# Second attention: the next group's scores in front of all four turned probabilities

## The chip, the cores and the metric

One core of one Trainium2 chip runs the whole kernel. The metric is the device time in microseconds (us) of one execution; lower is better. The engines are TensorE (matmuls), ScalarE (activations), VectorE and GpSimd (elementwise and reductions), and SyncE (issues most transfers). Each works through its own queue in order and waits on semaphores.

## The reference

Six layers are added to a state x of 16 batches x 64 tokens x 512 channels: a projected cross attention, a recurrent time mix, an FP4 feed-forward layer, a second cross attention without projections, a sparse self attention and a ternary feed-forward layer. The change touches the fourth:

```
q = layernorm(x), heads: 16 of 32 channels          # 64 tokens in each of 16 batches
k = v = ctx_1024, heads: 16 of 32 channels          # 512 keys in each of 16 batches
scores  = einsum('bhqd,bhkd->bhqk', q, k) / sqrt(32)
weights = softmax(scores, axis=-1)
x = x + einsum('bhqk,bhkd->bhqd', weights, v)
```

## The kernel before, in words

The layer is `cross_attention`. Its work is cut into 32 groups (`QUADS`), k = 0 to 31; batch b = k // 2, half = k % 2. A group is eight heads of one batch, held as four blocks r = 0 to 3 of 128 rows (two heads of 64 tokens each) by 512 keys; the title's "four heads" are these four blocks. For each group:

- `scores(k)` (matmul on L1116): 16 matmuls into four PSUM banks, one for each r. It waits until all four maxima of group k-1 are taken (`scored` at 4k), since they read the same banks.
- `scored_max(k)` on VectorE (L1250): four instructions, each copies a bank to SBUF (`l1x_prob`) and takes the row extremum (`l1x_negmax`). It waits for `scores(k)`.
- `exponential(k, r)` on ScalarE (L1201): one for each r, with the row sums, after the maximum of that r.
- `turn_probabilities(k, r)` on TensorE (L1131): four transposes of 128x128 into one of three banks, after exponential r and after the copy of the turn three before, which had the same bank.
- `turned_copy(k, r)`: the copy of a turned block to SBUF (`l1x_PT`), on ScalarE (L1209) for r = 0 and 2, and r = 1 of odd k; on VectorE (L1258) for r = 3, and r = 1 of even k.
- `half_product(k)` on TensorE (L1151): 64 small matmuls with the values, one group later.
- For odd k: `heads_copy` (ScalarE, L1214), `turn_back` (TensorE, L1161) and `finish_heads` (VectorE, L1273) of the batch before; GpSimd (L1101) adds the result to x.

The order in each queue is written out by hand in the loops over k. On ScalarE: exponentials 0 and 1, heads_copy (odd k), copy 0, exponential 2, copy 1 (odd k), exponential 3, copy 2. On VectorE: copy 3 of group k-1, finish_heads (odd k), copy 1 (even k), the four maxima of group k+1, and for every fourth k the moments of x. SyncE loads the keys of a batch (`l1x_KT`, three buffers, released by `score_full`) and the values (`l1x_ctx`, four buffers, released by `half_full`). The last group is followed by its half product, a turn_back and the first transposes for the next stage.

Of the kernel before, what the change touches and what calls it, by code (L numbers as in the profile page):

```python
# [461 lines left out]
def head_of(half, e, r):  # L462

    return 4 * (2 * half + e) + r
# [578 lines left out]
QUADS = 2 * B  # L1043
# [16 lines left out]
def cross_attention(nc, g, d, w, loads, zeros):  # L1060
# [19 lines left out]
    with nc.Block() as block:  # L1080
        @block.sync
        def _(sp):
            context_loads(d, w, (2, 3))(sp)
            for b in range(B):
                if b + 3 < B:
                    sp.wait_ge(score_full, 2 * (b + 1))
                    sp.dma_start(w.KT[b % 3][:, :, :], d.ctxT[b + 3]).then_inc(keys_loaded[b % 3], 16)
                if b + 4 < B:
                    sp.wait_ge(half_full, 2 * b + 2)
                    sp.dma_start(w.ctx[b % 4][:, :, :], ctx_dram[b + 4]).then_inc(ctx_loaded[b % 4], 16)  # L1090
            loads(sp)
# [11 lines left out]
        @block.tensor  # L1103
        def _(pe):
            def scores(k):

                b, half = k // 2, k % 2
                if half == 0:
                    pe.wait_ge(keys_loaded[b % 3], 16 * (b // 3 + 1))
                if k > 0:  # L1110
                    pe.wait_ge(scored, 4 * k)
                for e in range(2):
                    c = 2 * half + e
                    for r in range(4):
                        rows = slice(32 * r, 32 * r + 32)
                        last = nc.tensor.matmul(score[r][e * T:(e + 1) * T, :], w.QT[rows, c, b * T:(b + 1) * T],  # L1116
                                                w.KT[b % 3][rows, c, :], start=True, stop=True)
                last.then_inc(score_full, 1)

            def turn_probabilities(k, r):  # L1120

                n = 4 * k + r
                if n == 2:
                    pe.wait_ge(last_summed, 1)
                pe.wait_ge(exp_done, n + 1)
                if n >= 3:
                    pe.wait_ge(scalar_copied, SCALAR_COPIES[n - 3])
                    if VECTOR_COPIES[n - 3] > 0:
                        pe.wait_ge(vector_copied, VECTOR_COPIES[n - 3])
                for kc in range(KC):  # L1130
                    last = nc.tensor.transpose(probt[n % 3][:, kc * P:(kc + 1) * P], prob(k, r)[:, kc * P:(kc + 1) * P],  # L1131
                                               g.ident[:, :])
                last.then_inc(probt_full, 1)

            def half_product(k):

                b, half = k // 2, k % 2
                pe.wait_ge(scalar_copied, SCALAR_COPIES[4 * k + 3])
                pe.wait_ge(vector_copied, VECTOR_COPIES[4 * k + 3])
                if k == 0:  # L1140
                    pe.wait_ge(last_copied, 1)
                if half == 0:
                    pe.wait_ge(ctx_loaded[b % 4], 16 * (b // 4 + 1))
                    if b > 0:
                        pe.wait_ge(heads_done, b)
                for e in range(2):
                    c = 2 * half + e
                    for kc in range(KC):
                        for r in range(4):
                            h = head_of(half, e, r)  # L1150
                            last = nc.tensor.matmul(pv[32 * r:32 * r + 32, c * T:(c + 1) * T],  # L1151
                                                    w.ctx[b % 4][:, kc, h * HD:(h + 1) * HD],
                                                    turned(k, r)[:, kc * P + e * T:kc * P + (e + 1) * T],
                                                    start=kc == 0, stop=kc == KC - 1)
                last.then_inc(half_full, 1)

            def turn_back(b):

                pe.wait_ge(heads_out, b + 1)
                for half in range(2):  # L1160
                    last = nc.tensor.transpose(pv[:, 256 + half * P:256 + (half + 1) * P],  # L1161
                                               w.headsT[b % 2][:, half * P:(half + 1) * P], g.ident[:, :])
                last.then_inc(heads_back, 1)

            def turn_last_rows():

                pe.wait_ge(last_normed, 1)
                for c in range(CH):
                    ins = nc.tensor.transpose(pv[:, c * P:(c + 1) * P], g.XN[:, final, c * P:(c + 1) * P], g.ident[:, :])
                ins.then_inc(last_turned, 1)  # L1170

            scores(0)
            for k in range(QUADS):
                turn_probabilities(k, 0)
                turn_probabilities(k, 1)
                if k % 2 == 1 and k > 1:
                    turn_back(k // 2 - 1)
                if k + 1 < QUADS:
                    scores(k + 1)
                turn_probabilities(k, 2)  # L1180
                turn_probabilities(k, 3)
                if k > 0:
                    half_product(k - 1)
                else:
                    turn_last_rows()
            half_product(QUADS - 1)
            turn_back(B - 1)
            pe.wait_ge(scored, 4 * QUADS)
            for t in range(EARLY_TILES):
                pe.wait_ge(normed, t + 1)  # L1190
                for c in range(CH):
                    last = nc.tensor.transpose(score[t][:, c * P:(c + 1) * P], g.XN[:, t, c * P:(c + 1) * P], g.ident[:, :])
                last.then_inc(rows_turned, 1)
# [2039 lines left out]
```

## Time and profile before

| | |
|---|---|
| median of 3 runs | 1519.95 us (1519.93 to 1522.32) |
| time of the profiled execution | 1521.73 us |
| its span, first to last instruction | 1519.9 us |
| TensorE busy over the span | 1415.1 us (93%) |
| VectorE busy | 1106.7 us (73%) |
| ScalarE busy | 620.1 us (41%) |
| GpSimd busy | 176.2 us (12%) |
| mean granted TensorE clock | 0.986 |
| this stage, about | from 1112 to 1285 us |

The busy times are averages over six stages with different limits; a matmul's end is modelled, so a busy TensorE is not one at its peak. What this stage is limited by can only be read inside its stretch. Times in the timeline count from the span's start; entries of one kind that follow each other are merged, with their count behind an x. "issue" is idle time that nothing in the profile released.

### The profile page before, as it was taken

The numbers are of one execution on the slowest core, as the hardware profiler recorded it, in microseconds if no ns is written. First come the engines' busy times: TensorE is split into PE (matmuls) and PEld (weight loads), VectorE is DVE, ScalarE is ACT, GpSimd is POOL, SyncE is SP. The second block draws the span as 40 slices with busy tenths as digits, with TensorE's granted clock in tenths as the row PEclk, the third lists the DMA queues.
The fourth block names the chain that finished last, engine by engine and source line by source line (L and its number), as shares of the span: only waits on it lengthen the run. The fifth ranks groups of instructions, "written<-read, shape, count | busy, mean of one in ns | idle before, by whom it ended". The sixth has DMA issues, their size and how long they took to land. (4 is left out here: it accounts for less than half of the span.)

```text
span 1519.9 us, 33229 instructions
## 1 busy us (share of the span) xinstructions
PE 1415.1 (93%) x13858; PEld 929.3 (61%) x13858; DVE 1106.7 (73%) x2270; ACT 620.1 (41%) x1289; POOL 176.2 (12%) x171
## 2 busy tenths in 40 slices
PE   8999999999999999899979999999989998978898
PEld 5677777777777777434555644444446655667454
DVE  5577777877888788774565887677668777675787
ACT  2455444544544444111223411111178886134543
POOL 3300000000000000031000000000000001253800
PEclk9999999999999999899999999999999999999999
DMA  7353444444545543500006200000045563300000
GB/s 260 129 176 136 143 139 157 148 143 143 170 148 166 166 136 101 166 1 1 2 3 229 112 1 0 0 0 0 0 167 210 190 229 99 110 3 2 1 28 28
DMA packets 55449, 153.65 MB, mean 101 GB/s; under 512 B 11997, under 2 KB 16861, under 8 KB 49162
## 3 DMA queue, kind: packets, MB, share of 16 engines
q1 hardware_dynamic: 50186, 134.82, 26.0%
q0 software_dynamic: 5120, 16.78, 2.8%
q8 instruction: 107, 1.75, 0.5%
q14 instruction: 36, 0.29, 0.1%
HBM read 117.73 MB, written 33.85 MB: 100 GB/s over the span
## 5 line engine op out<-in xcount | busy, mean ns | idle before, releaser
L805 ACT ACTIVATE l0x_prob<-l0x_prob,l0x_negmax 128x512 f32<-128x512 f32 x128 | 90.9, 712 | 110.3 <-DVE l0x_negmax L881 110.2
L663 PE MATMUL bank<-l0x_upper_v,l0x_ctxT 128*128 128x512 f32 x256 | 106.6, 417 | 2.1 <-DVE l0x_V L860 2.1
L650 PE MATMUL bank<-l0x_ctxT,l0x_upper_k 128*128 128x512 f32 x256 | 106.7, 417 | 1.3 <-PEq L272 1.3
L665 PE MATMUL bank<-l0x_upper_v,l0x_ctxT_lower 128*128 128x512 f32 x256 | 101.6, 397 | 0.0
L664 PE MATMUL bank<-l0x_lower_v,l0x_ctxT 128*128 128x512 f32 x256 | 101.3, 396 | 0.0
L652 PE MATMUL bank<-l0x_ctxT,l0x_lower_k 128*128 128x512 f32 x256 | 100.7, 393 | 0.0
L651 PE MATMUL bank<-l0x_ctxT_lower,l0x_upper_k 128*128 128x512 f32 x256 | 100.2, 391 | 0.0
L2180 ACT ACTIVATE f_silu<-bank 128x512 f32<-128x512 f32 (+1 forms) x24 | 13.5, 561 | 190.4 <-PE bank L2107 190.4
L1201 ACT ACTIVATE l1x_prob<-l1x_prob,l1x_negmax 128x512 f32<-128x512 f32 x128 | 91.0, 715 | 0.0
L1131 PE MATMUL bank<-ident,l1x_prob 128*128 128x128 f32 x512 | 78.6, 288 | 13.2 <-ACT l1x_prob L1201 9.0
L1250 DVE CUSTOM_DVE_ANT_0 l1x_prob<-bank,l1x_zeros 128x512 f32<-128x512 f32 x128 | 80.8, 687 | 13.3 <-PE bank L1116 13.3
L608 POOL DMA_DIRECT2D turned_context<-l0x_whole x60 | 32.9, 548 | 475.6 <-ACT l0x_whole L783 475.6
L1131 PEld LDWEIGHTS bank<-ident,l1x_prob 128*128 128x128 f32 x512 | 55.6, 143 | 50.9 <-ACT l1x_prob L1201 41.7
L881 DVE CUSTOM_DVE_ANT_0 l0x_prob<-bank,l0x_mask 128x512 f32<-128x512 f32 x128 | 80.7, 687 | 3.8 <-PE bank L678 3.8
L2107 PE MATMUL bank<-f_gateT,f_x 128*128 128x512 f32 (+1 forms) x192 | 79.7, 558 | 1.4 <-ACT f_x L2172 1.4
L798 ACT ACTIVATE l0x_KT<-bank,columns 128x512 f32<-128x512 f32 x64 | 43.8, 684 | 91.0 <-PE bank L652 91.0
L2107 PE MATMUL bank<-f_upT,f_x 128*128 128x512 f32 (+1 forms) x192 | 79.5, 557 | 0.0
L2157 PE MATMUL bank<-f_downT,f_hT 128*128 128x512 f32 x154 | 67.4, 593 | 0.6 <-ACT f_hT L2191 0.6
L815 ACT ACTIVATE l0x_PT<-bank 128x512 f32<-128x512 f32 x128 | 65.9, 610 | 2.1 <-PE bank L687 2.1
L663 PEld LDWEIGHTS bank<-l0x_upper_v,l0x_ctxT 128*128 128x128 f32 x256 | 48.7, 190 | 24.5 <-issue 13.8
L650 PEld LDWEIGHTS bank<-l0x_ctxT,l0x_upper_k 128*128 128x128 f32 x256 | 48.1, 188 | 23.6 <-issue 14.2
L687 PE MATMUL bank<-ident,l0x_prob 128*128 128x128 f32 x512 | 62.3, 273 | 0.2
(339 smaller groups left out, 3091.7 us busy)
## 6 DMA issues: line engine op xcount, KB each, us to landing
l0x_ctx<-in_ctx SPq DMA_DIRECT2D x16, 1024.0 KB, 5.3
turned_context<-l0x_whole POOLq DMA_DIRECT2D x64, 256.0 KB, 2.4
l1x_KT<-turned_context SPq DMA_DIRECT2D x16, 1024.0 KB, 7.4
l1x_ctx<-in_ctx SPq DMA_DIRECT2D x16, 1024.0 KB, 4.9
fp_weight<-l0x_weight_piece SPq DMA_DIRECT2D x24, 352.0 KB, 4.8
f_raw<-fp_weight SPq DMA_DIRECT2D x3, 2816.0 KB, 18.3
l0x_abs_piece<-in_L_ffn_w_gate SPq DMA_DIRECT2D x16, 512.0 KB, 4.9
l0x_abs_piece<-in_L_ffn_w_up SPq DMA_DIRECT2D x16, 512.0 KB, 5.5
```

Of the source, the lines that this page charges most:

```text
L650: nc.tensor.matmul(bank[:, :], w.upper_k[:, kc, cols], c, start=kc == 0, stop=False)
L651: nc.tensor.matmul(bank[:, :], w.upper_k[:, kc, cols], c_lower, start=False, stop=False)
L652: last = nc.tensor.matmul(bank[:, :], w.lower_k[:, kc, cols], c, start=False, stop=kc == CH - 1)
L663: nc.tensor.matmul(bank[:, :], c, w.upper_v[:, kc, :], start=kc == 0, stop=False)
L664: nc.tensor.matmul(bank[:, :], c, w.lower_v[:, kc, :], start=False, stop=False)
L665: last = nc.tensor.matmul(bank[:, :], c_lower, w.upper_v[:, kc, :], start=False, stop=kc == CH - 1)
L805: nc.scalar.activation(w.prob[r][:, :], w.prob[r][:, :], ACT.Exp, scale=-1.0, bias=w.negmax[:, p:p + 1], accum_out=w.rowsum[:, b % 2, p:p ...
L881: nc.vector.tensor_tensor_reduce(w.prob[r][:, :], score[r][:, :], w.mask[b % 2][:, :], 1.0, 3e38, ALU.add, ALU.min, w.negmax[:, p:p + 1]). ...
L1131: last = nc.tensor.transpose(probt[n % 3][:, kc * P:(kc + 1) * P], prob(k, r)[:, kc * P:(kc + 1) * P], g.ident[:, :])
L1201: nc.scalar.activation(prob(k, r)[:, :], prob(k, r)[:, :], ACT.Exp, scale=-1.0, bias=w.negmax[:, p:p + 1], accum_out=w.rowsum[:, b % 4, p: ...
L1250: nc.vector.tensor_tensor_reduce(prob(k, r)[:, :], score[r][:, :], w.zeros[:, :], 1.0, 3e38, ALU.add, ALU.min, w.negmax[:, p:p + 1]).then_ ...
L2107: last = nc.tensor.matmul(bank[:, 0:n], w.x[:, kc, :], weight[:, kc, at:at + n], start=kc == 0, stop=kc == CH - 1)
```

## The change

In TensorE's loop the call `scores(k + 1)` moves from behind turns 0 and 1 of group k (and turn_back) to the front of the iteration. Each waits for what it waited for before; ScalarE's, VectorE's, SyncE's and GpSimd's queues keep their order.

```
             scores(0)
             for k in range(QUADS):
+                if k + 1 < QUADS:
+                    scores(k + 1)
                 turn_probabilities(k, 0)
                 turn_probabilities(k, 1)
                 if k % 2 == 1 and k > 1:
                     turn_back(k // 2 - 1)
-                if k + 1 < QUADS:
-                    scores(k + 1)
                 turn_probabilities(k, 2)
                 turn_probabilities(k, 3)
                 if k > 0:
```

## Rows read from the trace of the kernel before

**Rows 1.** Windows over the second attention: stretch, length, busy us (count) by engine, clock, DMA.
```profile
...
1112.00:1285.00 173.00, 152.01 (x3126) 100.90 (x3127) 136.17 (x376) 145.05 (x361) 12.65 (x11) 0.98 0.51 184
```

**Rows 2.** Waits in the same stretch: us in total, times, longest.
```profile
...
ACT l1x_PT L1209 <- PE bank L1131: 17.9, 27, 2.6
DVE l1x_prob L1250 <- PE bank L1116: 13.3, 31, 2.1
```

**Rows 3.** Timeline of TensorE (start us, us, line, operation, count, idle before).
```profile
...
1129.17 1.11 PE L1116 MATMUL bank<-l1x_KT,XNT 32*64 32x512 f32 x16
...
1163.24 1.09 PE L1131 MATMUL bank<-ident,l1x_prob 128*128 128x128 f32 x8
1164.17 0.38 PE L1161 MATMUL bank<-ident,l1x_headsT 128*128 128x128 f32 x2
1164.48 1.11 PE L1116 MATMUL bank<-l1x_KT,XNT 32*64 32x512 f32 x16
1165.53 0.66 PE L1131 MATMUL bank<-ident,l1x_prob 128*128 128x128 f32 x4
1166.47 0.66 PE L1131 MATMUL bank<-ident,l1x_prob 128*128 128x128 f32 x4 [0.29 <-ACT l1x_prob L1201]
1167.06 1.10 PE L1151 MATMUL bank<-l1x_PT,l1x_ctx 128*32 128x64 f32 x64
1168.09 1.09 PE L1131 MATMUL bank<-ident,l1x_prob 128*128 128x128 f32 x8
1169.11 1.11 PE L1116 MATMUL bank<-l1x_KT,XNT 32*64 32x512 f32 x16
...
1173.71 1.11 PE L1116 MATMUL bank<-l1x_KT,XNT 32*64 32x512 f32 x16
...
1270.37 1.11 PE L1116 MATMUL bank<-l1x_KT,XNT 32*64 32x512 f32 x16
```

**Rows 4.** The same timeline, a stall and the product behind it.
```profile
...
1201.15 0.92 PE L1131 MATMUL bank<-ident,l1x_prob 128*128 128x128 f32 x7 [1.88 <-issue]
1202.00 1.93 PE L1151 MATMUL bank<-l1x_PT,l1x_ctx 128*32 128x64 f32 x64
```

**Rows 5.** Timeline of ScalarE in the undisturbed pair.
```profile
...
1165.13 0.58 ACT L1209 ACTIVATE l1x_PT<-bank 128x512 f32<-128x512 f32 x1
1165.61 0.72 ACT L1201 ACTIVATE l1x_prob<-l1x_prob,l1x_negmax 128x512 f32<-128x512 f32 x1
...
1168.78 0.60 ACT L1209 ACTIVATE l1x_PT<-bank 128x512 f32<-128x512 f32 x1 [0.47 <-PE bank L1131]
1169.28 0.71 ACT L1201 ACTIVATE l1x_prob<-l1x_prob,l1x_negmax 128x512 f32<-128x512 f32 x1
...
1169.98 0.71 ACT L1201 ACTIVATE l1x_prob<-l1x_prob,l1x_negmax 128x512 f32<-128x512 f32 x1
```

**Rows 6.** Timeline of VectorE in the undisturbed pair.
```profile
...
1164.66 0.86 DVE L1273 TENSOR_TENSOR l1x_heads<-bank,l1x_rinv 64x256 f32<-64x256 f32 x2 [1.08 <-PE bank L1161]
...
1169.22 0.69 DVE L1258 COPY l1x_PT<-bank 128x512 f32<-128x512 f32 x1 [0.38 <-PE bank L1131]
1170.33 0.69 DVE L1250 CUSTOM_DVE_ANT_0 l1x_prob<-bank,l1x_zeros 128x512 f32<-128x512 f32 x1 [0.42 <-PE bank L1116]
...
1172.78 0.69 DVE L1258 COPY l1x_PT<-bank 128x512 f32<-128x512 f32 x1
```

**Rows 7.** Timeline of all engines in the last stage.
```profile
...
1426.23 0.75 DVE L2929 SCALAR_TENSOR_TENSOR f_h<-bank,f_worth,f_silu 128x512 f32<-128x512 f32 x1
...
1427.04 1.64 PE L2782 MATMUL bank<-f_gateT,f_x16T 128*128 128x512 bf16 x4 [2.67 <-DVE f_h L2929]
```

**Rows 8.** Windows, as in rows 1, of three stretches.
```profile
...
760.00:780.00 20.00, 14.62 (x558) 11.87 (x561) 11.01 (x18) 4.83 (x7) 0.00 (x0) 1.00 0.01 3
780.00:800.00 20.00, 14.23 (x385) 10.84 (x375) 17.08 (x34) 5.25 (x17) 0.00 (x0) 0.83 0.01 4
1200.00:1210.00 10.00, 8.85 (x176) 6.98 (x176) 6.21 (x19) 7.00 (x18) 1.28 (x1) 0.83 0.52 190
```

More of the change, by code:

```diff
@@ L1173, in _ @@
             for k in range(QUADS):
+                if k + 1 < QUADS:
+                    scores(k + 1)
                 turn_probabilities(k, 0)
@@ L1177, in _ @@
                     turn_back(k // 2 - 1)
-                if k + 1 < QUADS:
-                    scores(k + 1)
                 turn_probabilities(k, 2)
```

## The prediction

> **What bounds the kernel now.** I read the windows of the trace first, for the stage that the change touches. The second attention takes 173 us, 11.4% of the span. In it TensorE is busy 152 us, ScalarE 145 us and VectorE 136 us, at a granted clock of 0.98 [rows 1]: no engine is full, three are close, so the order of one group's steps sets the time. The list of waits comes next: ScalarE's copies wait 17.9 us for turned probabilities, VectorE's maxima 13.3 us for scores [rows 2]. Then TensorE's timeline. An undisturbed pair of groups (an even and an odd one) takes 1173.71 - 1164.48 = 9.23 us from one score block to the one two groups on; the 28 groups from the score block at 1129.17 to that at 1270.37 take 141.2 us, and 14 x 9.23 = 129.2 us, so 12.0 us are disturbance [rows 3]. Of what kind, TensorE's rows show: 1.88 us of "issue" (nothing in the profile released it), and behind it a product of 64 matmuls that takes 1.93 us where its like takes 1.10 us [rows 3, 4]; the window from 1200 to 1210 us has a mean granted clock of 0.83, so part of it ran at the lower level of 1.2 GHz [rows 8].
>
> In the undisturbed pair TensorE's own pitches are 1.05 us for a score block (1164.48 to 1165.53), 1.02 us for two turned heads (1168.09 to 1169.11), 1.03 us for a half product (1167.06 to 1168.09), 0.31 us for turn_back (1164.17 to 1164.48) [rows 3]. Twice (1.05 + 2 x 1.02 + 1.03) plus 0.31 is 8.55 us of the 9.23: TensorE hardly waits, because scores(k+1) stands between turns 1 and 2. While TensorE runs that block, ScalarE copies turn 0 and does exponential 2, VectorE copies turn 1 (even k) or finishes heads (odd k). These are hidden behind 1.05 us of scores.
>
> **The change part by part.** No instruction is added or removed. 31 score blocks of 16 matmuls move ahead of two turns (eight transposes); nothing moves on ScalarE, VectorE, SyncE or GpSimd. It costs by what now waits on what. I write t for the time from the start of a moved score block, scores(k+1).
>
> New wait: this block needs all four maxima of group k. They were complete long before it when it followed turns 0 and 1; now turns 0 and 1 of group k, which need only exponentials 0 and 1, are queued behind that wait, and behind them the rest of TensorE, ScalarE's copy 0 with exponentials 2 and 3 after it, and VectorE's copy 1 with the maxima of group k+1 after it.
>
> Even k, through VectorE. Turn 0 starts at 1.05. VectorE's copy of turn 1 starts 1.13 after turn 0 (1168.09 to 1169.22 [rows 3, 6]), at 2.18. It has the maxima's duration, 0.69, and I give it their pitch, 0.61 (a quarter of 2.45, below [rows 6]), so the four maxima start at 2.79. The scores themselves would have let them start at 1.22 (1169.11 to 1170.33 [rows 3, 6]): the earlier scores buy nothing, since the maxima are queued behind the copy. Four maxima have a pitch of 2.45 in all (1170.33 to 1172.78), the last starts 1.84 after the first and takes 0.69 [rows 6]. From a VectorE result to a TensorE start that waited for it no row of this stage speaks; the nearest is of the last stage, 1426.23 + 0.75 to 1427.04, 0.06 us [rows 7]. Bounds are 0 and 0.17 (ScalarE's exponential of 0.71 us, released to its turn 0.86 after its start, 1165.61 to 1166.47, is 0.15 past its end [rows 3, 5]); I take 0.06. First maximum to next score block: 1.84 + 0.69 + 0.06 = 2.59. Sum 5.38 us.
>
> Even k, through ScalarE. Copy 0 starts 0.69 after turn 0 (1168.09 to 1168.78), exponential 2 after 0.50, exponential 3 after 0.70 [rows 3, 5], turn 3 after 0.86, half product after 0.59 (1166.47 to 1167.06), the next score block 1.03 later: 1.05 + 0.69 + 0.50 + 0.70 + 0.86 + 0.59 + 1.03 = 5.42 us. The two loops are nearly equal; the longer counts, 5.42.
>
> Odd k, through VectorE. Turn_back starts 0.93 after turn 0 (1163.24 to 1164.17), finish_heads 0.49 later (1164.66), which takes 0.86 [rows 3, 6], then the maxima: 1.05 + 0.93 + 0.49 + 0.86 + 2.59 = 5.92 us. Through ScalarE the extra copy of turn 1 costs 0.48 (1165.13 to 1165.61 [rows 5]): 5.90 us. I take 5.92.
>
> A pair is then 11.34 us against 9.23, +2.11, and 14 pairs take 158.8 us. Both loops would have to be wrong for it to be less; with ScalarE's alone it is 11.32.
>
> The disturbances: 12.0 us before. TensorE now idles 11.34 - 8.55 = 2.79 us of each pair, so part of a stall falls into idle time, and it consumes instructions slower. Bounds are 0 (all hidden) and 12.0 (none); with a quarter of the time idle and stalls of up to 1.88 us against idle pieces of about 1 us, I take half, 6.
>
> The ends: four of the 32 groups lie outside the 28. Bounds are 1.0 us (only the two turns that now stand behind the last scores) and 4 x 2.11 / 2 = 4.2 us; the first groups have no turn_back and no half product of the group before, so I take 2.7.
>
> Transfers: a keys load is issued on a score block's end and used four groups later, about 18 us; an order moved by two turns (1.02 us) leaves that cover. Adds on GpSimd wait for finished heads only and are not waited for in the loop. Cost 0; if the cover were gone, TensorE would stand at the first score block of a batch, at most the 1.02 us moved, sixteen times.
>
> Sum: 158.8 + 6 - 141.2 + 2.7 = +26.3 us. The profiled execution has a span of 1519.9 us and its own time is 1521.73 us, 1.8 above the median of the runs, 1519.95; its sum would be 1548.0, and on the median 1546.3 us. I give the latter.
>
> **A rule weighed.** The transposes run at full clock here: the stage has a granted clock of 0.98 though two turned heads alternate with everything else [rows 1, 3]. The Trainium skill, page "TensorE: Matmul & The Clock Gate", Part 4, says that a transpose "doesn't count as PE-busy the same way" and that full clock does not engage for it. In this trace the rule does not show. By it the changed order, with 2.08 us of other matmuls left in 5.67, would sink to half clock, and the time would be that of the low clock rival below, the whole stage of it; since the trace speaks against the rule, it adds 0.02 to that rival's chance and no more (in the 0.10 below).
>
> **The rivals.**
> Low clock: TensorE's busy share falls to 8.55 / 11.34 = 75%. For it: the stretch 780 to 800 us has 14.2 us busy of 20 and a clock of 0.83. Against it: the stretch 760 to 780 us has 14.6 of 20 and a clock of 1.00 [rows 8], and the new idle pieces are about 1 us each. Price: at the lower clock a half product takes 1.93 us for 1.10 [rows 3, 4], a factor of 1.75; on the loop that adds 0.79 for scores, 0.38 each for turns 0 and 3 and 0.77 for the product, 2.3 us a group. A third of 28 groups gives +21, that is 1568 us; the whole stage +64. It decides from the point where the granted clock of the stage falls under about 0.9.
>
> No change: ScalarE's load would stay the bound (145 of 173 us) and the new wait be covered. That wants both loops of 5.4 to 5.9 us to be under 4.6, a whole score block less in each. Time 1520 us.
>
> Faster: one mechanism, VectorE's waits for scores. The 13.3 us [rows 2] vanish since scores come two turns earlier, the exponentials follow, and TensorE never waits for them: 1519.95 - 13.3 = 1506.7 us. It decides from the point where the maxima of k+1 may start at 1.22 and not 2.79 after the scores; the code's order on VectorE puts copy 1 or finish_heads in front, so only if these did not depend on turns issued behind the scores. They do.
>
> Half the loss: stalls vanish altogether and the ends cost 1.0: 158.8 - 141.2 + 1.0 = +18.6, and slack that I do not see (a shorter release, engines running ahead after each stall) takes another 5 to 8: about 1532 us.
>
> **How the numbers follow.** The forecast, with its own range from the bounds (+18.6 to 158.8 + 12 - 141.2 + 4.2 = +33.8: 1538.6 to 1553.8), 0.76. Low clock 0.10, half the loss 0.09, no change 0.03, faster 0.02. The range 1535 to 1558 takes the forecast's, some of the half loss and the mildest low clock: about 0.82. Changes under 0.2% (3 us) can't be told from none here. So faster 0.02, same 0.03, slower 0.95.
>
> **What would show it.** In the changed kernel's trace TensorE's score blocks lie 5.4 (even) and 5.9 us (odd) apart; before a score block TensorE waits for VectorE's maximum, a wait that is not in the list now, at least in odd groups; VectorE's maxima start 2.8 us after the score block and no longer wait for it, its copies and finish_heads wait for TensorE instead; ScalarE idles about 1.5 us before each copy 0. Sums of durations stay; the stage is about 199 us long. I am wrong if the score blocks lie under 5.2 us apart, if the granted clock of the stage falls under 0.9, or if time appears outside this stage.

## The result

The changed kernel takes 1544.54 us (median of 4 runs, 1541.35 to 1548.80) against 1520.93 us: a ratio of 1.0145, 95% interval 1.0129 to 1.0161, which is +22.1 us (19.6 to 24.5). The two medians by themselves are 23.6 us apart, inside that interval. The forecast was 1546.3 us, slower.

The windows of the kernel before, cut at the first score block of the stage, at that of the 4th group, at the last score block and at the stage's end; the fourth row is all that comes behind the stage (us, then busy us by engine in the order TensorE, its weight loads, VectorE, ScalarE, GpSimd, then clock, share of the DMA engines, GB/s):

```profile
...
1112.50:1129.17 16.67, 11.88 (x156) 7.14 (x157) 11.80 (x33) 12.30 (x29) 2.38 (x3) 0.90 0.67 253
1129.17:1270.37 141.20, 129.47 (x2717) 85.67 (x2716) 114.02 (x314) 121.89 (x309) 8.97 (x7) 0.99 0.54 195
1270.37:1284.47 14.10, 10.12 (x254) 7.77 (x253) 9.82 (x29) 10.86 (x25) 1.27 (x1) 1.00 0.01 3
1284.47:1519.90 235.43, 205.56 (x2240) 132.73 (x2240) 169.06 (x320) 87.15 (x124) 81.31 (x58) 0.98 0.11 37
```

The same windows of the changed kernel, cut at the same instructions:

```profile
...
1114.09:1132.63 18.54, 13.17 (x148) 7.64 (x149) 11.80 (x33) 11.76 (x27) 2.38 (x3) 0.72 0.57 227
1132.63:1292.17 159.54, 127.85 (x2723) 83.86 (x2716) 112.53 (x314) 121.17 (x310) 8.95 (x7) 1.00 0.48 173
1292.17:1308.34 16.17, 11.21 (x265) 8.64 (x261) 10.28 (x30) 11.37 (x27) 1.26 (x1) 1.00 0.01 3
1308.34:1547.00 238.66, 208.56 (x2240) 133.20 (x2240) 168.99 (x320) 87.10 (x124) 81.39 (x58) 0.96 0.11 37
```

The stage grew from 172.0 to 194.3 us, +22.3. The 28 groups in the middle give +18.3 (141.20 to 159.54), the first groups +1.9 and the tail behind the last scores +2.1. Busy times in the middle are nearly the same (TensorE 129.5 and 127.9 us), so nothing got more expensive: the engines wait. The granted clock of the middle is 1.00. The other 4.8 us by which this execution is longer lie outside the stage (1.6 ahead of it, 3.2 behind it), on the same instructions. This execution is the slowest of the four; of the 23.6 us between the medians the stage's 22.3 leave 1.3. The part behind the stage took 235.4 us at a granted clock of 0.98 in the kernel before and in e7 and e8 below, 238.6 to 238.9 at 0.96 here and in e1, e2 and e3, and 240.9 at 0.95 in e12, whose stage is the shortest of all; so its length doesn't go with that of the stage, and what sets it was not tested.

The list of waits of the changed kernel over the stage (us in total, times, longest):

```profile
...
ACT l1x_PT L1209 <- PE bank L1131: 43.2, 32, 2.6
PE bank L1131 <- ACT l1x_prob L1201: 35.3, 48, 1.0
DVE l1x_PT L1258 <- PE bank L1131: 26.8, 18, 3.3
DVE l1x_heads L1273 <- PE bank L1161: 17.1, 9, 1.9
...
PE bank L1116 <- DVE l1x_negmax L1250: 3.3, 1, 3.3
```

ScalarE's copies wait 43.2 us for turns instead of 17.9 [rows 2]; VectorE's copies and finish_heads now wait 26.8 and 17.1 us. VectorE's maxima wait for scores once more only, at the start (1.7 us; 13.3 us before [rows 2]): they now stand behind those copies. TensorE's timeline over an even and an odd group of the changed kernel:

```profile
...
1280.78 1.12 PE L1116 MATMUL bank<-l1x_KT,XNT 32*64 32x512 f32 x16
1281.82 1.09 PE L1131 MATMUL bank<-ident,l1x_prob 128*128 128x128 f32 x8
1283.87 1.36 PE L1131 MATMUL bank<-ident,l1x_prob 128*128 128x128 f32 x8 [0.95 <-ACT l1x_prob L1201]
1285.16 1.10 PE L1151 MATMUL bank<-l1x_PT,l1x_ctx 128*32 128x64 f32 x64
1286.23 1.12 PE L1116 MATMUL bank<-l1x_KT,XNT 32*64 32x512 f32 x16
1287.28 1.09 PE L1131 MATMUL bank<-ident,l1x_prob 128*128 128x128 f32 x8
...
1289.32 0.66 PE L1131 MATMUL bank<-ident,l1x_prob 128*128 128x128 f32 x4 [0.73 <-ACT l1x_prob L1201]
1290.51 0.66 PE L1131 MATMUL bank<-ident,l1x_prob 128*128 128x128 f32 x4 [0.53 <-ACT l1x_prob L1201]
1291.10 1.10 PE L1151 MATMUL bank<-l1x_PT,l1x_ctx 128*32 128x64 f32 x64
1292.17 1.12 PE L1116 MATMUL bank<-l1x_KT,XNT 32*64 32x512 f32 x16
```

The reader compares with [rows 3]: there a wait stands only in front of turn 3 (0.29 us); here TensorE waits 0.95 us for exponential 2 in each even group and 0.73 and 0.53 us in each odd one. From score block to score block it is 5.45 us (even k) and 5.94 us (odd k). ScalarE's copies 0 of the same pair, and VectorE's copy 1 (1282.95), finish_heads (1288.70), first and last maxima:

```profile
...
1282.52 0.60 ACT L1209 ACTIVATE l1x_PT<-bank 128x512 f32<-128x512 f32 x1 [1.55 <-PE bank L1131]
...
1287.97 0.60 ACT L1209 ACTIVATE l1x_PT<-bank 128x512 f32<-128x512 f32 x1 [1.14 <-PE bank L1131]
```

```profile
...
1282.95 0.69 DVE L1258 COPY l1x_PT<-bank 128x512 f32<-128x512 f32 x1 [1.04 <-PE bank L1131]
1283.56 0.68 DVE L1250 CUSTOM_DVE_ANT_0 l1x_prob<-bank,l1x_zeros 128x512 f32<-128x512 f32 x1
...
1285.39 0.69 DVE L1250 CUSTOM_DVE_ANT_0 l1x_prob<-bank,l1x_zeros 128x512 f32<-128x512 f32 x1
...
1288.70 0.86 DVE L1273 TENSOR_TENSOR l1x_heads<-bank,l1x_rinv 64x256 f32<-64x256 f32 x2 [1.90 <-PE bank L1161]
1289.59 0.69 DVE L1250 CUSTOM_DVE_ANT_0 l1x_prob<-bank,l1x_zeros 128x512 f32<-128x512 f32 x1
...
1291.42 0.69 DVE L1250 CUSTOM_DVE_ANT_0 l1x_prob<-bank,l1x_zeros 128x512 f32<-128x512 f32 x1
```

The first maximum starts 2.78 us after the score block (1283.56 - 1280.78), though the scores are there after 1.2. In the odd group the last maximum (1291.42, 0.69 long) ends 0.06 us before the next score block; the half product in front of that block started 1.07 us before it, where its pitch is 1.03: both loops close within hundredths of a microsecond. In the even group the last maximum (1285.39, 0.69 long) ends 0.15 us before the next block (1286.23).

### The profile page after: what moved, and what is told of

Read it like the earlier page. It is cut to its first block and busy times, and to the rows that moved or that the text cites. A ratio compares the mean times of both kernels' runs of the same rounds, so it can differ in the third digit from the quotient of the medians.

```text
span 1547.0 us, 33229 instructions
## 1 busy us (share of the span) xinstructions
PE 1421.0 (92%) x13858; PEld 929.0 (60%) x13858; DVE 1105.7 (71%) x2270; ACT 619.4 (40%) x1289; POOL 176.4 (11%) x171
## 5 line engine op out<-in xcount | busy, mean ns | idle before, releaser
L1131 PE MATMUL bank<-ident,l1x_prob 128*128 128x128 f32 x512 | 78.6, 288 | 36.1 <-ACT l1x_prob L1201 35.3
L1209 ACT ACTIVATE l1x_PT<-bank 128x512 f32<-128x512 f32 x80 | 47.6, 594 | 43.8 <-PE bank L1131 43.2
## 6 DMA issues: line engine op xcount, KB each, us to landing
f_raw<-fp_weight SPq DMA_DIRECT2D x3, 2816.0 KB, 18.3
```

## The experiments

All ratios are to the kernel before, run on the same chip; it took 1521.2 to 1522.9 us there, up to 2 us more than in the comparison above, so experiments are compared with each other by ratio and by pair, not by time. "28 groups" is the time from the 4th group's score block to the last one; "disturbed" is what is left of it after 14 undisturbed pairs.

| kernel | pair (even + odd), us | 28 groups | disturbed | ratio (95%) |
|---|---|---|---|---|
| before | 9.23 | 141.2 | 12.0 | 1 |
| changed | 5.45 + 5.94 | 159.5 | 0.1 | 1.0145 (1.0129 to 1.0161) |
| e1_maxima_first | 5.41 + 5.94 | 159.4 | 0.5 | 1.0139 (1.0107 to 1.0172) |
| e2_exp2_first | 5.46 + 5.94 | 159.5 | 0.0 | 1.0136 (1.0105 to 1.0166) |
| e3_both | 4.71 + 5.94 | 150.0 | 0.9 | 1.0073 (1.0049 to 1.0097) |
| e4_wait_alone | 4.83 + 5.05 | 138.4 | 0.1 | 1.0004 (0.9989 to 1.0020) |
| e5_no_loads_before | 9.21 | 129.0 | 0.1 | 0.9901 (0.9878 to 0.9925) |
| e6_no_loads_changed | 11.40 | 159.6 | 0.0 | 1.0158 (1.0141 to 1.0175) |
| e7_between_turns | 5.02 + 5.51 | 147.4 | 0.0 | 1.0041 (1.0025 to 1.0056) |
| e8_product_earlier | 8.98 | 137.9 | 12.2 | 0.9965 (0.9949 to 0.9981) |
| e9_finish_between | 4.71 + 5.19 | 140.4 | 1.8 | 1.0000 (0.9983 to 1.0017) |
| e10_spread_loads | 9.21 | 144.0 | 15.0 | 1.0041 (1.0027 to 1.0055) |
| e11_spread_and_product | 8.98 | 135.5 | 9.8 | 0.9973 (0.9962 to 0.9983) |
| e12_apart_and_product | 8.98 | 125.7 | 0.0 | 0.9896 (0.9877 to 0.9915) |

### One loop or two: e1, e2, e3

e1, VectorE's queue of the changed kernel:

```
                 if k > 0:
                     turned_copy(k - 1, 3)
+                if k + 1 < QUADS:
+                    scored_max(k + 1)
                 if k % 2 == 1 and k > 1:
                     finish_heads(k // 2 - 1)
                 if not copied_by_scalar(k, 1):
                     turned_copy(k, 1)
-                if k + 1 < QUADS:
-                    scored_max(k + 1)
```

> The changed kernel, with VectorE's four maxima of group k+1 put in front of finish_heads (odd k) and of copy 1 (even k). Theory A (two loops tie, one through VectorE of 5.38 and 5.92 us, one through ScalarE of 5.42 and 5.90 us): only the VectorE loop is shortened, to 1.22 + 2.59 = 3.8 us; the ScalarE loop keeps the pair at 11.3 to 11.4 us, the time stays at 1543 to 1546 us. Rival B (the wait for the maxima alone makes the loss, ScalarE only follows): the pair falls to about 9.9 us, the time to 1522 to 1530 us.

Measured: a pair of 11.35 us, 1545.95 us. Shortening the loop through VectorE alone gains next to nothing. The even group of 5.41 us is ScalarE's loop by itself (5.42 worked out). The odd group of 5.94 us is not quite that: the edit puts finish_heads behind the maxima, and that makes a new loop of 5.94 us, 0.04 more than ScalarE's 5.90 (more on it under e3). TensorE still waits 0.73 and 0.53 us for exponentials in it, as in the changed kernel.

e2, ScalarE's queue of the changed kernel:

```
-                turned_copy(k, 0)
                 exponential(k, 2)
+                turned_copy(k, 0)
```

> The changed kernel, with ScalarE's exponential 2 put in front of copy 0. Theory A: only the loop through ScalarE is shortened, by 0.70 us a group, to 4.7 and 5.2 us; the loop through VectorE keeps the pair at 11.3 us, the time stays at 1542 to 1545 us. Rival C (ScalarE's chain copy 0, exponential 2, exponential 3, turn 3, half product alone makes the loss): the pair falls to 9.9 us, the time to 1522 to 1530 us.

Measured: 5.46 + 5.94 = 11.40 us, 1543.40 us. This is VectorE's loop by itself. Shortening ScalarE's loop alone gains nothing either, but the wait moves into sight. In the changed kernel TensorE waited for a maximum in front of scores once (3.3 us); in e2:

```profile
...
PE bank L1116 <- DVE l1x_negmax L1250: 23.4, 30, 3.3
```

e3 has both edits.

> The changed kernel with both orders changed: maxima first on VectorE, exponential 2 before copy 0 on ScalarE. Theory A: now both loops are shorter and the pair falls to 9.9 us (ScalarE loop 4.72 and 5.20 us), which takes 14 x 1.48 = 21 us and some 2 us at the ends off 1544.5, to about 1522 us, plus what comes back of TensorE's issue stalls (0 to 12 us): 1521 to 1533 us. Rival D (a score block in front of the turns costs its own 1.05 us a group whatever stands behind it): the pair stays at 9.23 + 2.1 = 11.3 us and the time at 1544 us.

Measured: 4.71 + 5.94 = 10.65 us (9.9 expected), 1532.51 us. The even group falls to the 4.72 us worked out for it: there each of the two loops alone had held it up. The odd group doesn't move. TensorE's timeline of e3 (odd group from 1195.28 to 1201.22):

```profile
...
1195.28 1.11 PE L1116 MATMUL bank<-l1x_KT,XNT 32*64 32x512 f32 x16
...
1200.19 1.10 PE L1151 MATMUL bank<-l1x_PT,l1x_ctx 128*32 128x64 f32 x64 [0.67 <-DVE l1x_heads L1273]
1201.22 1.11 PE L1116 MATMUL bank<-l1x_KT,XNT 32*64 32x512 f32 x16
...
1205.93 1.11 PE L1116 MATMUL bank<-l1x_KT,XNT 32*64 32x512 f32 x16
```

The product waits 0.67 us for `l1x_heads`: finish_heads, now behind four maxima, holds back the half product of the next batch, which writes into the same bank. This is a third loop, 1.22 + 2.45 + 0.24 + 0.86 + 0.14 + 1.03 = 5.94 us, and the edit made it: in the changed kernel finish_heads stands in front of the maxima, ends at 1289.56 and is not what the product at 1291.10 waits for.

### The third loop cut: e9

e9 is e3 with finish_heads between the second and third maximum (`scored_max` takes the blocks it is to do):

```
+                if k + 1 < QUADS:
+                    scored_max(k + 1, range(2))
                 if k % 2 == 1 and k > 1:
                     finish_heads(k // 2 - 1)
+                if k + 1 < QUADS:
+                    scored_max(k + 1, range(2, 4))
                 if not copied_by_scalar(k, 1):
                     turned_copy(k, 1)
```

> The changed kernel with exponential 2 before copy 0 and the maxima first on VectorE, but finish_heads between the second and the third maximum. With all four maxima in front of finish_heads, odd groups stayed at 5.94 us since half_product waited for finish_heads (1.22 + 2.45 + 0.24 + 0.86 + 0.14 + 1.03). Theory A: this third loop is cut, odd groups fall to 5.2 us (ScalarE's loop), the pair from 10.64 to 9.9 us, the time by 10 us to 1520 to 1525 us. Rival D (a score block in front costs its own 1.05 us): no fall under the 10.6 us.

Measured: 4.71 + 5.19 = 9.90 us, 1523.44 us, ratio 1.0000. With the scores still in front of all four turns, the loss in time is gone. In the loop it is not gone: the pair stays 0.67 us above the 9.23 of the kernel before, 9.4 us in 28 groups, which is ScalarE's shortened loop (4.72 + 5.20); that the time comes out even is because only 1.8 of the 12 us of disturbance are left. 1.49 of the 2.16 us of loss a pair went with three edits that leave the score block where it is, so that much is the price of what is queued behind it on the other two engines, and rival D (2.1 us a pair whatever stands behind) falls.

### The wait alone, and half the way: e4, e7

e4, TensorE's queue of the kernel before:

```
             for k in range(QUADS):
+                if k + 1 < QUADS:
+                    pe.wait_ge(scored, 4 * (k + 1))
                 turn_probabilities(k, 0)
```

> The kernel before, scores left where they were; only the wait for all four maxima of group k is put in front of turn 0 of group k, where the changed kernel has it. Theory A: VectorE's copy 1 and finish_heads are still hidden behind the score block, so the loop is turns 1.02 + first maximum 1.22 + 2.59 = 4.83 us (even) and 5.14 us (odd, with turn_back), a pair of 9.97 us, that is +0.74 x 14 = 10 us with the ends about 11; if the slack swallows the issue stalls of 12 us as it did in the changed kernel, the time is 1519 to 1523 us, if not up to 1532. Rival B (the wait alone makes the loss): a pair of 11.4 us and 1544 us.

Measured: a pair of 9.88 us. TensorE's timeline:

```profile
...
1163.68 1.11 PE L1116 MATMUL bank<-l1x_KT,XNT 32*64 32x512 f32 x16
...
1168.51 1.11 PE L1116 MATMUL bank<-l1x_KT,XNT 32*64 32x512 f32 x16
...
1172.32 1.09 PE L1131 MATMUL bank<-ident,l1x_prob 128*128 128x128 f32 x8 [0.40 <-DVE l1x_negmax L1252]
...
1173.56 1.11 PE L1116 MATMUL bank<-l1x_KT,XNT 32*64 32x512 f32 x16
```

From 1163.68 to 1168.51 it is the 4.83 us worked out for an even group, from 1168.51 to 1173.56, with turn_back in it, 5.05 (5.14 worked out), and the new wait is seen at 1172.32. Undisturbed, the wait costs 0.65 us a pair, 9 us in 28 groups; the disturbances of 12 us are gone with it, and the time is that of the kernel before (1.0004), so rival B falls. The other 1.51 us of the changed kernel's pair come with the scores standing in front of the turns.

e7 puts scores(k+1) between turn 0 and turn 1 of the kernel before:

```
                 turn_probabilities(k, 0)
+                if k + 1 < QUADS:
+                    scores(k + 1)
                 turn_probabilities(k, 1)
                 if k % 2 == 1 and k > 1:
                     turn_back(k // 2 - 1)
-                if k + 1 < QUADS:
-                    scores(k + 1)
```

> The kernel before with scores(k+1) between turn 0 and turn 1, halfway to the changed order. Theory A: VectorE loop with t from turn 0: even 0.51 + 1.05 to turn 1, copy 1 at 2.18, first maximum at 2.79, next score block at 5.38 and turn 0 0.51 earlier: 4.87 us; odd the same with turn_back 5.4 us; a pair of 10.3 us, +1.1. If the slack swallows the 12 us of stalls: 14 x 10.3 = 144 against 141.2 us, with the ends +4 to +5 us: 1523 to 1527 us. Rival D (the loss is the block's own 1.05 us in front of turn 0): no loss of the pair, 9.23 us, and 1520 us.

Measured: score blocks of e7 at

```profile
...
1154.90 1.12 PE L1116 MATMUL bank<-l1x_KT,XNT 32*64 32x512 f32 x16 [0.42 <-DVE l1x_negmax L1250]
...
1160.41 1.12 PE L1116 MATMUL bank<-l1x_KT,XNT 32*64 32x512 f32 x16
...
1165.43 1.12 PE L1116 MATMUL bank<-l1x_KT,XNT 32*64 32x512 f32 x16 [0.42 <-DVE l1x_negmax L1250]
```

5.51 us (odd) and 5.02 us (even), a pair of 10.53 us, 1529.69 us. TensorE waits 0.42 us for a maximum in front of the block that ends each even group. Half the way costs more than half the loss (1.30 of 2.16 us), and more than was expected (10.3 us and 1523 to 1527 us); rival D (9.23 us) falls. The even group is 0.15 us longer than worked out (4.87). 0.09 of that is the release: the last maximum ends 0.15 us before the block at 1165.43 (1164.59, 0.69 long), not 0.06. The rest was not looked into.

### Where the 12 us of disturbance went: e5, e6

e5 takes the loads of keys and values out of the kernel before, e6 out of the changed one; the waits stay, and the two waits on the loads are for the first load of each buffer:

```
                 if b + 3 < B:
                     sp.wait_ge(score_full, 2 * (b + 1))
-                    sp.dma_start(w.KT[b % 3][:, :, :], d.ctxT[b + 3]).then_inc(keys_loaded[b % 3], 16)
                 if b + 4 < B:
                     sp.wait_ge(half_full, 2 * b + 2)
-                    sp.dma_start(w.ctx[b % 4][:, :, :], ctx_dram[b + 4]).then_inc(ctx_loaded[b % 4], 16)
```

> The kernel before without the 25 loads of keys and values that SyncE issues inside the loop of the second attention (batches 3 and up read the keys of earlier ones, 4 and up the values; this part of the computation is left out, all waits on score and product blocks stay). It asks what the 12 us of issue stalls are. Theory E (TensorE's instructions arrive late because 1 MB loads share the DMA engines): no stalls, score blocks at 1129 and 1270 us lie 129 to 131 us apart, the time is 1508 to 1511 us. Rival F (they are TensorE outrunning its own supply, whatever else is moved): 141 us apart and 1520 us.

Measured: 129.0 us for the 28 groups and no "issue" in front of any matmul of them, 1510.25 us. The stalls come with the loads, and rival F falls.

> The changed kernel without the same 25 loads of keys and values inside the second attention (that part of the computation is left out). Its trace shows no issue stalls that the loads could have caused, so both theories of the stalls say: pair 11.4 us, time unchanged at 1542 to 1546 us. A fall by more than 3 us would say that the loads cost something in the new order after all.

Measured: 159.6 us for the 28 groups, as in the changed kernel; 1547.52 us (1.5 above the range expected), ratio 1.0158 (1.0141 to 1.0175), whose interval overlaps that of the changed kernel. In the middle of the changed order the loads cost nothing.

What the gaps are can be read further from their places. Counted through TensorE's program from the first score matmul, the nine gaps marked "issue" in the kernel before stand in front of matmuls 414, 538, 786, 1158, 1408, 1531, 2152, 2277 and 2524, from the first all whole steps of 124 (within three). Those of e8 and e10 stand on the same grid, and so do the few that are left in e1, e3 and e9. The DMA queue of the instructions in the kernel before over the stage (packets, MB, share of the time of 16 engines):

```profile
...
q8 instruction: 25, 0.41, 1.0%
```

25 packets for the 3126 matmuls and 3127 weight loads [rows 1] are one for 125 matmuls. So the gaps stand a whole number of packets apart, at nine of the 22 such places in the 28 groups, as late instructions would. The nine last 8.2 us together; the rest of the 12 us is slower work behind them.

### A faster kernel: e8, e10, e11, e12

e8, TensorE's queue of the kernel before:

```
                 turn_probabilities(k, 2)
-                turn_probabilities(k, 3)
                 if k > 0:
                     half_product(k - 1)
-                else:
+                turn_probabilities(k, 3)
+                if k == 0:
                     turn_last_rows()
```

> The kernel before with half_product(k-1) between turns 2 and 3 and not behind turn 3. The kernel before waits 0.3 to 0.5 us a pair for exponential 3 in front of turn 3, and ScalarE 0.67 us for turn 0 behind the product. The product fills that wait: the pair falls from 9.23 to 8.7 to 8.9 us (ScalarE is busy 8.67 us of it), 14 x 0.4 = 6 us less; 1513 to 1517 us if the stalls stay as they are. Rival G: with less slack the stalls grow by as much, and the time stays at 1521 us.

Measured: 8.98 us a pair (8.7 to 8.9 expected), 1518.12 us, 12.2 us of stalls, ratio 0.9965. A gain of 3.5 us in the loop, where 6 were expected; rival G falls.

e10 cuts each load in four and issues the parts over the pair (TensorE's waits on the loads count the parts):

```
+                for j in range(4):
...
+                    if b > 0 and b + 3 < B:
+                        sp.wait_ge(exp_done, 4 * (2 * b + (2, 3, 3, 4)[j]) + (4, 2, 4, 2)[j] - 4)
...
+                    for c in (2 * j % 4, 2 * j % 4 + 1):
+                        if j < 2 and b + 3 < B:
+                            sp.dma_start(w.KT[b % 3][32 * c:32 * c + 32, :, :], d.ctxT[b + 3][32 * c:32 * c + 32]).then_inc(keys_loaded[b % 3], 16)
```

> The kernel before with each 1 MB load of keys or values cut into four of 256 KB (32 partitions each, so packets keep their size), issued two at a time at four points of a pair, about two exponentials (2 us) apart, where one load of keys and one of values went out together. The same bytes. Theory E1 (a burst delays TensorE's instructions, and shorter bursts delay them less than its slack): stalls fall from 12 to 0 to 6 us, score blocks 1129 to 1270 lie 129 to 135 us apart, 1509 to 1516 us. Rival E2 (it is the bytes in flight over the stage that count, or the wait for one packet in each of the queues): 141 us apart, 1521 us.

Measured: 144.0 us for the 28 groups, stalls of 15.0 us, 1528.05 us, worse than either theory said. The DMA queue over the stage (packets, MB, share of the time of 16 engines), in the kernel before and in e10:

```profile
...
q1 hardware_dynamic: 10480, 31.36, 49.6%
```

```profile
...
q1 hardware_dynamic: 11680, 31.37, 78.2%
```

The same bytes hold the engines for 78% of the time instead of 50%. A part of 256 KB takes 5.0 (values) to 6.2 us (keys) to land, a whole of 1024 KB takes 4.9 to 7.4, all medians. The cut hardly shortened a burst, it filled the gaps between them.

> The same spread loads together with half_product(k-1) between turns 2 and 3, which by itself gave a pair of 8.98 us with 12.2 us of stalls left over 28 groups. If E1 holds: 14 x 8.98 + 0 to 6 = 126 to 132 us for the 28 groups, 1505 to 1512 us, the fastest of all. If E2 holds: 138 us and 1516 us.

Measured: ratio 0.9973 (0.9962 to 0.9983), 1518.06 us, 135.5 us for the 28 groups, 9.8 us of stalls: between the two theories, and not told apart from e8. E1 falls.

e12 is e8 with whole loads, but one after the other:

```
                     sp.wait_ge(score_full, 2 * (b + 1))
+                    sp.wait_ge(exp_done, 8 * (b + 1))
```

> half_product(k-1) between turns 2 and 3, as in the fastest kernel so far (0.9965 of the kernel before, pair 8.98 us, 12.2 us of stalls), and the keys load of a batch waits for the exponentials of group 2b+1, so that it goes out a group (4.6 us) apart from the values load and not 0.4 us from it. Loads stay whole, so their share of the DMA engines should stay near 50% (cutting them raised it to 78% and the stalls did not fall). Theory E3 (a stall needs two loads stacked in front of the instruction transfer): stalls fall to 0 to 6 us, ratio 0.989 to 0.994. Rival E2 (one load in flight is enough): stalls stay at 9 to 14 us, ratio 0.995 to 0.998.

Measured: 125.7 us for the 28 groups, which is 14 x 8.98 with nothing left; 1507.39 us, ratio 0.9896 (0.9877 to 0.9915), faster than both kernels. The DMA engines were busy 65% of the 28 groups, against 54% in the kernel before, and not near 50% as expected; so it is not the share of time or the bytes in flight that make the stalls, and rival E2 falls. SyncE's issues in the kernel before (one pair's worth) and in e12:

```profile
...
1203.97 0.33 SPq L1090 DMA_DIRECT2D l1x_ctx<-in_ctx  x1
1204.35 0.43 SPq L1087 DMA_DIRECT2D l1x_KT<-turned_context  x1
```

```profile
...
1195.99 0.33 SPq L1088 DMA_DIRECT2D l1x_KT<-turned_context  x1
1201.30 0.33 SPq L1091 DMA_DIRECT2D l1x_ctx<-in_ctx  x1
1204.97 0.33 SPq L1088 DMA_DIRECT2D l1x_KT<-turned_context  x1
```

A values load and a keys load went out 0.38 us apart and then nothing for most of a pair; now they are 3.7 to 5.3 us apart. The stage is 15.7 us shorter than in the kernel before (156.3 us for 172.0); this execution gave 5.5 us of that back behind the stage (240.9 us for 235.4), at the granted clock of 0.95 named above. TensorE's timeline of e12, with the product in front of turn 3 and no wait between:

```profile
...
1181.59 0.66 PE L1132 MATMUL bank<-ident,l1x_prob 128*128 128x128 f32 x4
1182.18 1.10 PE L1152 MATMUL bank<-l1x_PT,l1x_ctx 128*32 128x64 f32 x64
1183.21 1.79 PE L1132 MATMUL bank<-ident,l1x_prob 128*128 128x128 f32 x12
```

## Why the prediction was right

**The two loops.** Even 5.42 worked out, 5.45 measured; odd 5.92 and 5.94; pair 11.34 and 11.39; 14 pairs 158.8 and 159.5 us. The sum through VectorE and that through ScalarE were said to be nearly equal. e1, e2 and e3 show it for the even group: 5.41 us with ScalarE's loop alone, 5.46 with VectorE's alone, 4.71 with neither. For the odd group e2 shows VectorE's alone (5.94); ScalarE's 5.90 is seen in TensorE's waits for exponentials, and that neither is left at 5.19 us is shown by e9, since e1 and e3 had made a third loop of their own. One choice between the two was the wrong way round: in even groups the prediction let ScalarE's 5.42 count over VectorE's 5.38. The release of 0.06 us from a maximum to the score block, taken from the last stage, was 0.06 in odd groups (1291.42 + 0.69 to 1292.17) and 0.15 in even ones (1285.39 + 0.69 to 1286.23), inside its bounds of 0 and 0.17 (the two rows named for 0.17 give 0.14); with 0.15 VectorE's loop is 5.47 and the longer one. The error of 0.09 was covered by the tie.

**The disturbances** are the term that was mis-sized: I kept 6 of 12 us, and none were left in the 28 groups. The argument with idle pieces of about 1 us against stalls of up to 1.88 left too much. In e4 a pair of 9.88 us is already enough to lose them all, in e9 one of 9.90 us keeps 1.8 us. That alone accounts for -6 us.

**The ends** were 3.9 us for the 2.7 taken (bounds 1.0 and 4.2). The tail's 2.1 us is the same with and without loads (16.17 us in e6). A part of the opening's 1.9 is clock: its granted clock went from 0.90 to 0.72. e6, the same order without the loads, has an opening 1.4 us shorter at 0.90:

```profile
...
1111.88:1129.00 17.12, 10.77 (x149) 6.07 (x149) 11.79 (x33) 11.76 (x27) 2.37 (x3) 0.90 0.47 185
```

TensorE stands 3.3 us for the first maxima in both, and 3.1 us for the first exponential in the kernel before at 0.90, so that stand alone doesn't make the low clock; what does stays open.

Together: 18.3 + 3.9 = +22.3 us before rounding, for the +26.3 forecast. The medians are 23.6 us apart, so some 1.3 us lie outside the stage, and the kernel before took 1520.93 us and not the 1519.95 the forecast started from. These two, 2.3 us, hide part of the 4 us by which the stage was overestimated: 1544.5 against 1546.3 is closer than the sum deserves.

**The rivals.** Low clock: the middle ran at 1.00 with TensorE busy 80% of it, so it fell for the loop; only the opening, 19 us long, was lower (0.72). By the rule of the Trainium skill that it was weighed with (page "TensorE: Matmul & The Clock Gate", Part 4, on transposes) the clock would have sunk; the middle of this stage does not agree with it, at 1.00. Half the loss had its stalls right (they vanished) and no slack beside: the loops are as long as worked out. No change and faster fell with the loops; the maxima do start 2.78 us after the scores, behind copy 1, and putting them first (e1) does not help by itself.

**What was to be seen.** Score blocks 5.4 and 5.9 us apart, ScalarE's idle before copy 0 (1.55 and 1.14 us) and the missing wait of the maxima were as written. One was not: a wait for a maximum in front of each odd score block. There was only the first one, of 3.3 us; the two loops end within hundredths of a microsecond, and TensorE's idle time is booked further up, in front of turns 2 and 3 (35.3 us in the list of waits). The stage is 194 us long, not 199. The prediction also called itself wrong if time appeared outside the stage: in the profiled execution 4.8 us did, between the medians about 1.3. It had no term for it, and the rows say only that the granted clock behind the stage was 0.96 for 0.98.

What stays open: why stacked loads cost 12 us at a pair of 8.98 to 9.23 us and 0 to 1.8 at 9.88 and more. It is not the spacing: the changed kernel and e4 issue the two loads as close together, 0.37 us apart. That a slower TensorE leaves its instruction supply time to catch up is argued, not shown. Nor was the e12 spacing tried on the order of the kernel before alone, nor was e1 with finish_heads kept out of the third loop.

## What to carry to other kernels

Where three engines pass a ring of buffers around, sum each loop from row to row before moving a block on one of them; a block that looks free in its own queue may be the cover for a copy on another engine. When two loops tie, relieving one shows nothing, and the list of waits names only one of them: undo both at once, and sum again the loops of the order that this makes, since it can hold a third.

Before reordering compute against unexplained "issue" gaps, look at when the large loads are issued: moving one load by half a period took the ratio from 0.9965 (e8) to 0.9896 (e12), more than the only order of matmuls that gained here.

## What the runs showed of the hardware

Stalls of TensorE with no releaser (up to 1.88 us, 12 us in 28 groups) come and go with loads of 1 MB on the same core: 0.1 us of disturbance without them (e5), 12 with two issued 0.38 us apart, 0 with the two 3.7 to 5.3 us apart (e12), 15 with the same bytes in parts of 32 partitions (e10). They stand at fixed places of the program, whole steps of 124 matmuls apart, and the instruction queue moved one packet for 125 matmuls. Parts of 256 KB on 32 partitions landed in 5.0 to 6.2 us, hardly sooner than four times as much on 128, and raised the queue's share of engine time from 49.6% to 78.2%.
